# The two mixings of a pair ahead of its two output tiles on TensorE

## What is computed

```python
proj = hidden_states @ in_proj_w.T
gate, xBC, dt = jnp.split(proj, [INTER, INTER + CONV_DIM], axis=-1)
conv = causal_conv4(xBC) + conv_b
x, Bm, Cm = jnp.split(silu(conv), [INTER, INTER + NG * SS], axis=-1)
# per head, in chunks of 128 tokens:
scores = (C . B) * exp(cs[l] - cs[s]) * (l >= s)
y = scores @ (x * dt) + carried state + x * D
yg = y * silu(gate)
out = yg * rsqrt(mean(yg ** 2 over a group) + eps) * norm_w
return out @ out_proj_w.T
```

## Time and profile before

| | us |
|---|---|
| median of three runs | 1516.63 |
| the profiled execution | 1516.77 |
| its span in the trace | 1515.0 |
| PE busy | 1475.2 (97% of the span) |
| DVE busy | 1294.3 (85%) |
| POOL busy | 1154.9 (76%) |
| ACT busy | 1017.0 (67%) |

### The profile page before, as it was taken

How to read it: one execution, slowest core, us unless ns; L and a number is a source line. 1 busy time by engine, 2 the same in 40 slices (tenths; PEclk the granted TensorE clock), 3 DMA queues, 4 the chain that set the end, 5 groups by cost and what they waited for, 6 DMA issues and landing times. The chain is left out here.

```text
span 1515.0 us, 24359 instructions
## 1 busy us (share of the span) xinstructions
PE 1475.2 (97%) x7720; PEld 1210.0 (80%) x7720; DVE 1294.3 (85%) x1663; ACT 1017.0 (67%) x2155; POOL 1154.9 (76%) x917
## 2 busy tenths in 40 slices
PE   6979899999999999999999999999999999999999
PEld 4767788888888888888888888888888888888767
DVE  6689987998789987999789987998789987998675
ACT  4367777666776677667766777667766777667650
POOL 3017997699858997699958998699958997699850
PEclk9989999999999999999999999999999999999999
DMA  3026552444425442544434442544424442444211
GB/s 126 1 84 191 185 154 91 154 160 147 147 93 166 148 152 91 153 156 155 143 94 165 153 152 87 160 153 154 139 100 159 153 155 84 160 161 140 86 40 56
DMA packets 165679, 198.77 MB, mean 131 GB/s; under 512 B 21040, under 2 KB 86576, under 8 KB 165296
## 3 DMA queue, kind: packets, MB, share of 16 engines
q1 hardware_dynamic: 165552, 197.22, 40.4%
HBM read 160.98 MB, written 36.18 MB: 130 GB/s over the span
## 5 line engine op out<-in xcount | busy, mean ns | idle before, releaser
L167 PE MATMUL bank<-h_hi,mx_w_hi 128*128 128x512 f32 x1152 | 457.9, 397 | 6.0 <-POOL mx_w_lo L918 4.7
L168 PE MATMUL bank<-h_lo,mx_w_hi 128*128 128x512 f32 x1152 | 449.2, 390 | 0.0
L169 PE MATMUL bank<-h_hi,mx_w_lo 128*128 128x512 f32 x1152 | 448.5, 389 | 0.0
L974 DVE SCALAR_TENSOR_TENSOR mx_acc<-bank,mx_cw,mx_acc 128x510 f32<-128x510 f32 (+2 forms) x480 | 353.9, 745 | 43.2 <-ACT mx_acc L959 30.0
L1606 DVE TENSOR_TENSOR mx_mix<-mx_mix,mx_cbt 128x1536 f32<-128x1536 f32 x128 | 266.4, 2086 | 35.9 <-ACT mx_mix L1415 35.9
L1405 ACT ACTIVATE mx_mix<-mx_csb,ncs 128x256 f32<-128x256 f32 x512 | 218.2, 500 | 111.1 <-PE bank L1826 109.1
L1281 POOL TENSOR_TENSOR mx_y<-mx_y,mx_sg 128x512 f32<-128x512 f32 x126 | 245.9, 1972 | 21.9 <-DVE mx_y L1614 21.9
L167 PEld LDWEIGHTS bank<-h_hi,mx_w_hi 128*128 128x128 f32 x1152 | 216.4, 188 | 57.5 <-POOL mx_w_lo L918 5.6
L169 PEld LDWEIGHTS bank<-h_hi,mx_w_lo 128*128 128x128 f32 x1152 | 216.4, 188 | 46.1
L168 PEld LDWEIGHTS bank<-h_lo,mx_w_hi 128*128 128x128 f32 x1152 | 216.7, 188 | 42.2
L918 POOL TENSOR_TENSOR mx_w_lo<-mx_w_raw,mx_w_hi 128x512 fp32r<-128x512 f32 x144 | 191.1, 1328 | 72.6 <-ACT mx_w_hi L913 71.9
(11 more groups left out here) (193 smaller groups left out, 2244.3 us busy)
## 6 DMA issues: line engine op xcount, KB each, us to landing
mx_csb<-cs_rows SPq DMA_DIRECT2D x128, 512.0 KB, 4.2
mx_w_raw<-in_w_in SPq DMA_DIRECT2D x144, 256.0 KB, 3.6
x_squares<-mx_th SPq DMA_DIRECT2D x128, 256.0 KB, 2.0
mx_xd<-x_squares SPq DMA_DIRECT2D x512, 64.0 KB, 2.0
mx_wo_raw<-in_w_out SPq DMA_DIRECT2D x64, 256.0 KB, 4.2
res<-in_x SPq DMA_DIRECT2D x8, 256.0 KB, 4.0
out<-res SPq DMA_DIRECT2D x8, 256.0 KB, 2.0
f_base_raw<-in_base_wt SPq DMA_DIRECT2D x1, 1024.0 KB, 7.0
```

The lines of the kernel that those rows point to most:

```text
L167: nc.tensor.matmul(out, w_hi, x_hi, start=first, stop=False)
L168: nc.tensor.matmul(out, w_hi, x_lo, start=False, stop=False)
L169: return nc.tensor.matmul(out, w_lo, x_hi, start=False, stop=last)
L974: self.nc.vector.scalar_tensor_tensor(dst, src[:, :, 0:SEQ - k], self.cw[:, c, TAPS - 1 - k:TAPS - k], dst, ALU.mult, ALU.add).then_inc(s[ ...
```

## The change

In `pair` on PE, the loop over the mixings stands ahead of the loop over the output tiles. Nothing else is edited; the other engines' instructions stand as they did, and PE has the same instructions in another order.

```diff
                 for st in steps:
                     project_gate(g, st)
+                for st in steps:
+                    mix_tokens(g, st)
                 for p in steps:
                     if has_tile(g, p) and not (g == NG - 1 and p == STEPS - 1):
                         project_out(g, p)
-                for st in steps:
-                    mix_tokens(g, st)
```

## The result

The changed kernel took 1575.47 us (median of 4 runs, 1574.39 to 1577.06), the kernel before 1516.57 on the same chip: the ratio is 1.0385, 95% interval 1.0372 to 1.0397. It is slower, as forecast, but by 58.9 us instead of 31, and outside the range.

What follows compares the result with a forecast made beforehand. The prediction took PE, busy 97% of the span and without slack mid-run, to bound the kernel. Its four terms, 13 + 2 + 14 + 2 = 31 us, added to 1516.8 gave 1548 us, range 1535 to 1566.

Steps and rivals of the forecast that it cites:

- term 3: j = 7 of groups 0 to 6: later ACT decays make the second make_mix miss its mixing's slot; 14 us (8 to 18).
- term 2: j = 2 to 4: later output tiles delay DVE's adds, skip_y, then POOL's gating, splits and scaling; 2 us (0 to 7).
- term 4: Last pair of all: output tile no longer covers the wait for POOL's scaling, partly offset by POOL starting sooner; 2 us (0 to 3).
- Term 1: First pairs of groups 1 to 7: scaled x comes too late for the earlier mixings; 13 us (10 to 16).
- The path through ACT's copy: End of a pair: ACT's copy of the second output tile delays the next pair's decays and first make_mix by 1.83 us.
- my case of 1.4: j = 7: the second make_mix comes before POOL's weight split and ends 1.4 us after the slot; taken in three of seven groups.
- my low end: j = 7: the second make_mix, moved by 1.83 us, ends 1.4 us after its mixing's slot.
- my 2.5: j = 7: POOL's weight split comes first, so the second make_mix ends 2.5 us late; taken in four of seven groups.
- The clock's: Rival: PE's granted clock falls at each of 14 new stalls, 24 us more, 1572 us; chance 0.04.
- Each pair longer, 1566 or above: Rival: delays through output tiles and ACT reach their upper bounds, lengthening each pair; 49 us, 1566 us; chance 0.10.
- Only the start pays: Rival: only groups' starts cost much, as j = 7 absorbs ACT's later decay; 17 us, 1534 us; chance 0.14.
- not slower: Rival: earlier mixings move the decay, make_mix and scaling round ahead, so inputs are ready; 1515 to 1519 us; chance 0.06.

Runs made afterwards that it cites:

- scale_first: The changed kernel with POOL's two scalings of x in j = 1 to 4 moved ahead of that pair's gating and splits; 1587.3 us.
- adds_later: The changed kernel with DVE's add_quads and add_group of a pair moved behind the next pair's skip_y's; 1559.4 us.
- bias_early: The changed kernel with only DVE's smaller conv constant (L944) moved ahead of the first make_mix of j = 7; 1559.3 us.
- constants_early: The changed kernel with both of DVE's conv constants moved ahead of the first make_mix of j = 7; 1547.6 us.

## Why the prediction was wrong in size

The direction, the places and the engines were right: no pair got shorter by more than 0.1, PE's new idle time stands ahead of L1822 alone, j = 5 and 6 cost nothing (-0.3), and every term has its stalls where it put them. The steps that failed are L944 carried over at its old length and the clock put at nothing (term 3), the two times of term 2 that nearly met, and a gain that did not come (term 4):

- **Term 1**, first pairs: 13 forecast (10 to 16), 15.4 measured, 9.9 in j = 0 and 5.5 in j = 1. Right within its bounds, and by its working: the delay of j = 0 does count towards that of j = 1. In group 3 the second scaling of j = 1 ended at T + 15.2 before (T = 627.02); now it ends at T + 13.0 (662.54, T = 649.54), 2.2 earlier, since T itself comes later by the 2.1 that j = 0 lost, and j = 1 pays 0.7 where I had read 2.6. Both pairs together pay 15.3 in groups 1 to 7, 0.3 a group more than the 13.2 that I had read off the second pairs. That is about the slot, 0.14 earlier than I had it (term 2), and some 0.1 for each pause; this is an estimate from those rows. What each delay comes from differs: x that has not landed in j = 0, POOL's queue in j = 1 (scale_first).
- **Term 2**, j = 2 to 4: 2 forecast (0 to 7), 11.1 measured, 9.5 of it in groups 1 to 7. The loop is the one described (adds_later takes it away). The step that failed is the comparison of two times that nearly met: I had the scaling's end at T + 12.6 and the slot at T + 12.55, 0.1 a pair; they are at T + 12.66 and T + 12.41, and PE pays some 0.1 more for the pause itself. Most of the 0.14 in the slot is that a pair no longer begins with a change of type: its first matmul takes 0.39 (1122.09) where it took 0.50. That makes 0.39 a pair in j = 2 and 3. In j = 4 it is 0.54, by a path that I did not have: there the same loop delays `make_mix` b, and POOL's scaling lengthens it by 0.8. My upper bound of 0.35 was too low for all three.
- **Term 3**, j = 7 of groups 0 to 6: 14 forecast (8 to 18), 26.7 measured, of which 18.9 are stalls and 7.8 the clock. The path through ACT's copy came out as worked: `make_mix` a is 1.83 later. Two steps failed. First, the stall costs 2.7 a group: `make_mix` b did come ahead of POOL's weight split, my case of 1.4, but I carried L944 over at the 0.16 that it took before, and it takes 1.34. With L944 out of the way a pair pays 1.42 (bias_early), my low end; so L944 is the step, 1.3 a group. I had priced the port for the long instruction and not for the two short ones ahead of it. That PE's idle time, 2.44, lies near my 2.5 is luck: the 2.5 was for a split that comes first. Nor did the split stay at T + 11.99, as I had assumed; it comes at T + 13.65, behind ACT's rounding. Second, the clock, which I put at nothing: 1.55 to 1.60 in five groups, 7.8.
- **Term 4**, last pair: 2 forecast (0 to 3), 5.9 measured. The uncovered tile, 2.8, is there. The gain that I set against it, POOL's chain starting sooner, is not. In the changed kernel POOL's gating does start at T - 1.4 instead of T + 0.8, but POOL then waits 3.04 for ACT's rounding, which stands behind the later decays; the mixing starts at T + 10.29, and at T + 10.00 before. And the mixings at 1.2 GHz add 2.3.
- **The rivals.** The clock's was right in kind, with a chance of 0.04. My argument against it was that the wait in group 0 (3.1 of idle PE) was longer than any stall I forecast; the clock fell in five of seven stalls of 2.44, which are shorter than that wait and no longer than the 2.5 I forecast. It took 7.8 + 2.3 = 10 us, a sixth of the loss. Its price of up to 1.7 a fall was right (1.55). That its 1572 lies near the measured time is luck: it put 24 us on the clock, at all 14 stalls, and none of the stalls of the first pairs (up to 1.75 of idle PE) brought a fall in groups 1 to 7. Each pair longer, 1566 or above, came true in its time and for terms 2 and 3, but j = 5 and 6 did not stretch. Only the start pays, and not slower, fell with the 26.7 of j = 7: the constants passed later, not sooner.

Sum: 15.4 + 11.1 - 0.3 + 26.7 + 5.9 - 0.4 (between the groups) = 58.4, of which the forecast had 31. The errors are independent in place. Those of term 2 and of L944 are of one kind: two times, or two engines' requests, that nearly met, taken at the favourable side.

The Trainium skill ("SBUF — State Buffer", section "Who interferes with whom") says that VectorE's `tensor_scalar`, too, can enter modes that use both port pairs, and that it and GpSimd then block each other, the one that comes later for the whole of the other's instruction. The trace agrees: L944, a TENSOR_SCALAR, takes 1.34 where it ends with a split of 1.31, and 0.16 where it is done at once. I had drawn on that page for `make_mix` alone.

## What to carry to other kernels

When one engine is at 100% and the others only just keep up, moving its work ahead of a long independent block spends the slack of every loop that runs through that block; look for the loop in the pair before the one that stalls, and follow each queue from there instruction by instruction, the short ones too. Where a forecast rests on two times within a few tenths of a microsecond, or on which of two engines comes first, take the unfavourable case into the sum, not only into the range. And price a stall on TensorE with what it does to the clock behind it.

## What the runs showed of the hardware

- An instruction of 128 x 10 elements on VectorE (L944) took 0.16 us in the seven groups of the kernel before and 1.33 to 1.34 in those of the changed one, and in both it started within 0.01 us of one of POOL's splits. Beside POOL's mask of 0.64 it took 0.16 or 0.66 (constants_early).
- Which of `make_mix` and POOL's weight split is first was decided by 0.1 to 0.5 us, and the second paid for most of the first: `make_mix` 1.75 and the split 2.41, or the split 1.27 and `make_mix` 2.77.
- Stalls of equal length, 2.44 us, brought the granted clock down in 17 of 28 pairs j = 7 of four runs, of 1.18 in none of 7, of 4.05 in all of 7. A fall cost some 1.55 us of later work where the stall itself had cost 2.7.
